# Two layers of attention and feed-forward on one core: the first chunk scored without rows over DRAM, weights folded on column tiles, late weights as steps, a low-rank product on row tiles

## Chip, core and metric

One core of a Trainium2 chip runs the whole program in one launch. The metric is device time in microseconds (us), the median of some runs. TensorE is called PE below, VectorE DVE, ScalarE ACT, GpSimd POOL, and SP is the sync engine, which here only issues DMAs.

## The reference, cut to what matters

The input is 16 sequences of 256 tokens with 128 features. Four stages follow one another, each with a residual and a layer norm: A0 (causal attention, 16 heads of 8 dimensions, queries and keys from low-rank products), F0 (a gated feed-forward of width 512 with two hidden layers), A1 (attention without mask), F1 (a feed-forward in which a router picks one of 8 low-rank additions).

```
q = einsum('bhtr,hrd->bhtd', einsum('btd,hdr->bhtr', x, q_a), q_b)   # rank 64, k alike
att = softmax(where(causal, q @ k.T / sqrt(8), min)); y = att @ v
x = layernorm(x + y @ o_w.T + o_b)                                   # A0
h = silu(x @ w1.T * s1) * (x @ w2.T * s2)
h = gelu(h @ h1.T * t1); h = gelu(h @ h2.T * t2)
x = layernorm(x + h @ w3.T * s3)                                     # F0
x = layernorm(x + attention(x @ W_qkv + b) @ W_out + b_out)          # A1, no mask
e = argmax(x @ gate_W.T + gate_b)
h = relu(x @ wi.T + wi_b + (x @ A[e].T) @ B[e].T)
x = layernorm(x + h @ wo.T + wo_b)                                   # F1
```

## The kernel before

**Chunks and steps.** A chunk is one sequence of 256 tokens, and each of the four stages handles 16 chunks. Every engine runs a list of steps written out by hand as letters (`SEQUENCE`): `KIND` gives each letter's name and stage, and a letter's n-th use is chunk n. Engines meet through counted semaphores. All PSUM banks are one pool of eight, and `BANK_TABLE` says which bank each step of PE takes, so a step waits until that bank's last user is done.

**Weights at the start.** PE folds the low-rank factors into the two 128x128 matrices `wq`: 16 products, one for a pair of heads and a side (queries, keys), each with a 128x128 stationary operand (`wqa`) and 16 moving columns (`wqb`) (L821). DVE copies the result (L626). ACT issues the DMAs of all other weights at the start, but for `wh` and `w3`, which follow the first chunk's key rows (`key_rows`, L544 to L550).

**Scores in bf16 rows.** Attention scores have a contraction of only 8, and float32 precision is wanted. So `qk` gives q and k for all heads (features by tokens); ACT and DVE split them into three bf16 parts (`split`, L557, L659 to L669); SP parks the parts in a DRAM scratch (`park`, L423) and fetches them back as 72 rows a head (`fetch`: `qrow` L434, `krow` L439), so that one bf16 matmul with 72 rows holds all products of the parts. `pass1` (L874, L883) makes scores with queries on partitions, 3 banks for 4 heads in A0 and 4 in A1, and DVE takes the row maxima (L704, or L695 with the mask from chunk 2 on in A0; in chunks 0 and 1 PE adds the mask, L865). `maxima` turns the maxima (L894), DVE splits them too (L723 to L729), and SP writes them as three more rows of `qrow` (L447). `pass2` (L916) makes the transposed scores less the maximum with 75 rows, ACT takes the exponential (L575), POOL zeroes the diagonal's upper part in A0 (`causal`, L515), and `values` (L934) multiplies by v on four column tiles of 32. For chunk 0 of A0 the maxima and rows go in two halves (`HALVED`, `early`, L902 to L715, L453).

**The rest of a chunk.** `outputs`, `merge`, `project`, `turn` normalise, turn and project; the feed-forward of F0 is `gated` (L985), `hidden` (L1003, half of all its PE work), `down` (L1052). `scale` multiplies F0's weights by their scales on DVE (L636 to L648), once. In F1, `route` (L1014) gives the router's logits and the low-rank values, DVE keeps those of the chosen expert in `low`, `lora` turns them (L1023), and `expert` adds, for each of four blocks of 128 features, the product with `wi` (L1033) and one with `wlb` (L1034). Of the latter's 128 contraction rows only 32 hold weights, the rest are zero.

## Time and profile before

| | |
|---|---|
| median of 3 runs | 928.54 us (925.82 to 929.03) |
| the profiled execution | 927.51 us, span 925.7 us |
| PE busy | 870.4 us, 94% |
| PE weight loads | 689.3 us, 74% |
| DVE busy | 670.8 us, 72% |
| ACT busy | 488.5 us, 53% |
| POOL busy | 185.6 us, 20% |
| DMA | 65.17 MB, mean 70 GB/s |

The span runs from the first to the last instruction; some 1.8 us of the execution's time lie outside it. A busy share counts a matmul from its start to its modelled end, and neighbours overlap, so that PE at 94% is not PE at its peak. A float32 matmul shows as two records and a bf16 one as one, so counts of float32 matmuls in the views are double those in the code.

### The profile page before, as it was taken

What the parts mean: (1) busy time and instruction counts of PE and PEld (TensorE: products, weight loads), DVE (VectorE), ACT (ScalarE), POOL (GpSimd) and SP (SyncE); (2) the same over time, 40 slices, a digit from 0 to 9 for tenths busy, and PEclk for the clock granted to TensorE, in tenths of its full rate; (3) what the DMA queues carried; (4) which work ended last, traced back from release to release, by engine and by line L of the source; (5) the groups of instructions that cost most, each with busy time, mean ns of one, the idle gap of its engine ahead of it and who ended that gap; (6) DMA issues with size and microseconds to landing.
All of it is one profiled execution on the core that took longest, in us unless ns stands there. A gap on an engine that the chain in (4) does not pass through costs nothing.

```text
span 925.7 us, 19247 instructions
## 1 busy us (share of the span) xinstructions
PE 870.4 (94%) x7076; PEld 689.3 (74%) x7076; DVE 670.8 (72%) x2379; ACT 488.5 (53%) x951; POOL 185.6 (20%) x389
## 2 busy tenths in 40 slices
PE   5589899999999999999999999999999999999996
PEld 4358687876777876688777887778867888787855
DVE  5767658749998579964799659965899659654863
ACT  1143454376655545645547665646565665562372
POOL 2132221003400233002320034002320114010211
PEclk9879899999999999999999999999999999999999
DMA  7613031402322034301252023400442022002200
GB/s 243 205 47 104 20 98 53 126 13 60 105 71 77 1 93 129 87 2 37 68 145 76 2 70 113 116 10 1 118 115 71 7 75 65 13 8 63 81 15 12
DMA packets 49044, 65.17 MB, mean 70 GB/s; under 512 B 5624, under 2 KB 42744, under 8 KB 44248
## 3 DMA queue, kind: packets, MB, share of 16 engines
q1 hardware_dynamic: 46552, 58.02, 21.9%
q10 hardware_dynamic: 2400, 5.93, 1.9%
q8 instruction: 57, 0.93, 0.4%
q14 instruction: 35, 0.29, 0.1%
HBM read 48.46 MB, written 14.68 MB: 68 GB/s over the span
## 4 chain that ended last, share of the span: by engine, by line
PE 65%; DVE 12%; DMA 11%; issue 4%; ACT 4%; SPq 3%; POOL 1%; ACTq 0%; POOLq 0%; DVEq 0%
PE banks L1003 19%; PE banks L916 8%; PE banks L934 8%; DMA krow<-scratch 7%; PE banks L883 6%; PE banks L985 5%; PE banks L1052 4%; DVE top L704 3%; PE banks L838 2%; DMA scratch<-split 2%; DMA qrow<-tsplit 2%; SPq L439 1%; PE banks L874 1%; PE banks L1033 1%; PE banks L1034 1%
## 5 line engine op out<-in xcount | busy, mean ns | idle before, releaser
L575 ACT ACTIVATE prob<-banks 128x384 f32<-128x384 f32 (+1 forms) x512 | 247.0, 550 | 117.2 <-PE banks L916 97.4
L704 DVE TENSOR_REDUCE top<-banks 128x2 f32<-128x512 f32 (+1 forms) x280 | 176.0, 680 | 38.5 <-PE banks L883 27.9
L695 DVE CUSTOM_DVE_ANT_0 banks<-banks,above 128x128 f32<-128x128 f32 x448 | 145.5, 388 | 42.0 <-PE banks L883 29.6
L916 PE MATMUL banks<-qrow,krow 75*128 75x256 bf16 (+1 forms) x1024 | 155.6, 266 | 8.6 <-ACT prob L575 3.9
L883 PE MATMUL banks<-krow,qrow 72*128 72x256 bf16 x768 | 133.9, 277 | 9.2 <-DVE top L704 5.0
L916 PEld LDWEIGHTS banks<-qrow,krow 75*128 75x128 bf16 x1024 | 89.5, 100 | 47.0 <-ACT prob L575 11.2
L934 PE MATMUL banks<-prob,v 128*32 128x256 f32 (+1 forms) x2048 | 122.8, 367 | 0.7 <-POOL prob L515 0.6
L508 POOL TENSOR_TENSOR ln_rstd<-ln_var,minus_half 128x2 f32<-128x2 f32 x64 | 44.8, 703 | 380.6 <-DVE ln_var L764 380.3
L1003 PE MATMUL banks<-glu,wh 128*128 128x256 f32 x512 | 116.5, 381 | 1.0 <-ACT prob L575 1.0
L1003 PE MATMUL banks<-hid,wh 128*128 128x256 f32 x512 | 115.9, 380 | 0.0
L1003 PEld LDWEIGHTS banks<-glu,wh 128*128 128x128 f32 x512 | 94.9, 190 | 13.8 <-ACT prob L575 1.2
L1003 PEld LDWEIGHTS banks<-hid,wh 128*128 128x128 f32 x512 | 95.1, 190 | 12.7 <-ACT hid L597 0.5
L883 PEld LDWEIGHTS banks<-krow,qrow 72*128 72x128 bf16 x768 | 68.7, 99 | 33.9 <-DVE top L704 7.1
L934 PEld LDWEIGHTS banks<-prob,v 128*32 128x32 f32 x2048 | 56.6, 111 | 48.5 <-issue 18.1
L597 ACT ACTIVATE hid<-banks 128x512 f32<-128x512 f32 x64 | 38.2, 597 | 86.8 <-PE banks L1003 86.4
L515 POOL TENSOR_SCALAR_AFFINE_SELECT prob<-prob 128x512 f32<-128x512 f32 x128 | 81.9, 639 | 0.0
L513 POOL TENSOR_TENSOR pool_carrier<-minus_half 128x1 f32<-128x1 f32 x128 | 29.5, 230 | 242.2 <-ACT prob L575 241.6
L695 DVE DVE_READ_ACCUMULATOR2_ANT top<- 128x1 f32 x448 | 62.4, 139 | 0.0
L985 PE MATMUL banks<-xt,w 128*128 128x256 f32 x256 | 62.2, 389 | 0.0
L503 POOL TENSOR_TENSOR resid<-x,rows 128x256 f32<-128x256 f32 x48 | 34.9, 727 | 113.4 <-DVE ln_sum L751 104.7
L575 ACT ACT_TABLE_LOAD x35 | 44.9, 1283 | 16.6 <-PE banks L916 15.9
L985 PEld LDWEIGHTS banks<-xt,w 128*128 128x128 f32 x256 | 47.4, 194 | 6.8 <-ACT prob L575 0.4
(100 smaller groups left out, 1164.1 us busy)
## 6 DMA issues: line engine op xcount, KB each, us to landing
qrow<-scratch SPq DMA_DIRECT2D x30, 576.0 KB
krow<-scratch SPq DMA_DIRECT2D x90, 192.0 KB
scratch<-split SPq DMA_DIRECT2D x96, 128.0 KB, 1.9
xt<-in_xt SPq DMA_DIRECT2D x16, 128.0 KB, 2.4
x<-in_x SPq DMA_DIRECT2D x16, 128.0 KB, 2.7
wh<-in_wh ACTq DMA_DIRECT2D x2, 1024.0 KB, 8.5
out<-xout SPq DMA_DIRECT2D x16, 128.0 KB, 2.0
qrow<-tsplit SPq DMA_DIRECT2D x90, 8.0 KB
```

What stands on the lines that cost most here:

```text
L508: nc.gpsimd.tensor_tensor(ln_rstd[s][:], ln_var[s][:], minus_half[:], ALU.pow).then_inc(rstd[s], 1)
L515: nc.gpsimd.affine_select(out=diag, in_=diag, compare_op=ALU.is_ge, fill=0.0, base=0, pattern=[[0, 2], [0, QB], [1, P]], channel_multiplie ...
L575: nc.scalar.activation(prob[s][:, j % 2, g, 0:wide], banks[:, b, 0:wide], ACT.Exp, scale=1.0 / float(np.sqrt(np.float32(HD))) if s == A0 e ...
L597: nc.scalar.activation(hid[layer][:, 2 * m:2 * m + 2, :].rearrange("p m t -> p (m t)"), banks[:, g, :], ACT.Gelu).then_inc(gelued, 1)
L695: done = nc.vector.tensor_tensor_reduce(out=bank[:, g * wide:(g + 1) * wide], in0=bank[:, g * wide:(g + 1) * wide], in1=above[:, 2 * P - w ...
L704: nc.vector.tensor_reduce(out=dst, in_=src, axis=AX, op=ALU.max, negate=True).then_inc(maxed[s], 1)
L883: done = nc.tensor.matmul(at, queries(h, qb), keys(h, 2), start=True, stop=not masked, skip_group_check=True)
L916: done = nc.tensor.matmul(bank[:, kb * SEQ:(kb + 1) * SEQ - q0], krow[s][n % DEEP[s]][0:ROWSM, h, kb * P:(kb + 1) * P], qrow[s][n % DEEP[s ...
L934: done = nc.tensor.matmul(banks[32 * i:32 * i + 32, g, q0:SEQ], v[s][:, kb, GROUP * j + i, :], prob[s][:, j % 2, i, kb * SEQ:(kb + 1) * SE ...
L985: done = nc.tensor.matmul(banks[:, g, i * TOK:(i + 1) * TOK], w12[:, side, (2 * m + i) * P:(2 * m + i + 1) * P], xt[F0][n % AHEAD][:], sta ...
L1003: done = nc.tensor.matmul(banks[:, g, i * TOK:(i + 1) * TOK], wh[:, layer, k, (2 * m + i) * P:(2 * m + i + 1) * P], (glu, hid[0])[layer][: ...
L1052: done = nc.tensor.matmul(banks[:, g, t * D:(t + 1) * D], src[:, k, t * P:(t + 1) * P], w[:, k, :], start=k == 0, stop=k == HB - 1)
```

## The change

**First chunk of A0.** It no longer goes over DRAM. The folded weights are spread so that each head has 8 of 32 columns (`wex`), and four products a side give q and k of all heads with one head in 8 of each 32 partitions (L936). `qf` holds the queries of four heads at once; `kf[g]` holds only head g's keys, with zeros elsewhere and a one in a spare row, so that a float32 matmul with 128 rows gives one head's scores (L997, L1001; pass 2 L1065). The maxima are put into that spare row by `shift`: PE turns them and DVE adds them into `qf`. No split, park, fetch or rows of maxima remain for this chunk; chunk 1 is the first to be parked.

**Fold.** `wqb` is stationary (32 columns, padded with zeros) and `wqa` moves (128 columns), on four column tiles. The result is transposed, so it is copied, turned by PE (L928) and copied again. The input `qk_b` is twice as large.

**Late weights.** `late` is a step on ACT in three parts: scales and `w12`; `wh` and `w3`; all others. The first two stand ahead of all exponentials, the third behind six of them. DVE's memsets of `krow` are on POOL.

**Park and fetch.** Queries and keys have scratches of their own, the keys' in the order in which they are read. A park is six DMAs and was three; a fetch of keys is still three, each from one run of DRAM.

**Low-rank product.** `wlb` holds the 32 rows of weights twice, at partitions 0 and 32, and DVE writes `low` twice. An `expert` step now covers the whole chunk: all four products with `wi` first, ahead of the wait for `lowt`, then the four with `wlb`, each with 32 rows, alternating between the two row tiles and two banks.

**Order.** All five lists and the bank table are new throughout.

```diff
-HALVED = {A0: 0, A1: CHUNKS - 1}
+HALVED = {A0: None, A1: CHUNKS - 1}
+EARLY = {A0: 0, A1: CHUNKS - 1}
@@ SEQUENCE, pe: first line, before and after
-        "abaccccccccdcccceeefeeeeeggceccceeceecececcecccggbfhaijeeeeeeeeegeeekegeeesggbhcscaicctcjccccctcctfkcccc"
+        "aaaaaaabcaadeaeaeeeeafeegeeeefeeeeaaaaaafaaafaaahacgidjeeeeeeeekeefeeeeeferffchaaaridaaajsaasaakaaarrgasaa"
@@ pe, start
-            pe.wait_ge(weights0, 2 * DMA)
-            for pair in range(HEADS // 2):
-                if pair == HEADS // 4:
-                    pe.wait_ge(weights0b, DMA)
-                for side in range(2):
-                    at = banks[:, 0, side * D:(side + 1) * D].rearrange("p (c h) -> p c h", h=HEADS)[:, :, 2 * pair:2 * pair + 2]
-                    done = nc.tensor.matmul(at, wqa[:, pair, side, :],
-                                            wqb[:, pair, side, :].rearrange("p (c h) -> p c h", h=2), start=True, stop=True)
-            done.then_inc(folded, 1)
+            for half in range(2):
+                if half == 0:
+                    pe.wait_ge(weights0, 2 * DMA)
+                else:
+                    pe.wait_ge(weights0b, DMA)
+                for side in range(2):
+                    for i in range(4):
+                        pair = 4 * half + i
+                        done = nc.tensor.matmul(banks[32 * i:32 * i + 32, half, side * D:(side + 1) * D], wqb[:, pair, side, :],
+                                                wqa[:, pair, side, :], start=True, stop=True, skip_group_check=True)
+                done.then_inc(folded, 1)
             pe.wait_ge(made, 2)
+            for half in range(2):
+                pe.wait_ge(kept, half + 1)
+                for side in range(2):
+                    done = nc.tensor.transpose(banks[:, 2 + half, side * D:(side + 1) * D], turned[:, half, side * D:(side + 1) * D], ident[:])
+                done.then_inc(unturned, 1)
+            pe.wait_ge(wex_ready, 2)
+            pe.wait_ge(loaded[0], 2 * DMA)
+            for half in range(2):
+                for side in (1, 0):
+                    for i in range(2):
+                        done = nc.tensor.matmul(banks[:, 5 + 2 * half - side, i * TOK:(i + 1) * TOK], wex[:, side, 2 * half + i, :], xt[A0][0][:],
+                                                start=True, stop=True)
...
@@ pe, pass1
+                if s == A0 and is_first(n):
+                    for g in range(GROUP):
+                        if u == 0:
+                            at = bank[:, g * P:(g + 1) * P]
+                            nc.tensor.matmul(at, qf[:, j, 0:P], kf[g][:, j, 0:P], start=True, stop=False, skip_group_check=True)
+                            done = mask(at)
...
@@ dve, start
+            for half in range(2):
+                dve.wait_ge(folded, half + 1)
+                nc.vector.tensor_copy(turned[:, half], banks[:, half, 0:2 * D]).then_inc(kept, 1)
...
+            def shift(half, g):
+                at = qf[:, 2 * half:2 * half + 2].rearrange("p j t -> p (j t)")
+                nc.vector.tensor_tensor(at, at, banks[:, g, :], ALU.add).then_inc(shifted, 1)
@@ act
+            def late(s, n, k):
+                if k == 0:
+                    act.dma_start(early[:, HEADS * D:HEADS * D + 4 * HID], d_in["scales"].partition_broadcast(P)).then_inc(weights2, DMA)
+                    act.dma_start(w12[:], d_in["w12"]).then_inc(weights2, DMA)
+                elif k == 1:
+                    for layer, there in enumerate((weights3, weights4)):
+                        act.dma_start(wh[:, layer], d_in["wh"][:, layer]).then_inc(there, DMA)
+                    act.dma_start(w3raw, d_in["w3"]).then_inc(weights4, DMA)
...
@@ sp, park
-                    sp.dma_start(scratch[s][n % 2][:, i].rearrange("a p t -> p a t"), split[s][:, i]).then_inc(parked[s][n % 2], DMA)
+                    sp.dma_start(scratch[s][n % 2][i], split[s][:, i, 0]).then_inc(parked[s][n % 2], DMA)
+                    sp.dma_start(kscratch[s][n % 2][:, i], split[s][:, i, 1]).then_inc(parked[s][n % 2], DMA)
@@ pe, expert
-            def expert(s, n, m, g):
-                if m == 0:
-                    pe.wait_ge(lora_done, 1 * n + 1)
-                last.wait(pe, g)
+            def expert(s, n, ga, gb):
+                for pair, g in enumerate((ga, gb)):
+                    last.wait(pe, g)
+                    for i in range(2):
+                        m = 2 * pair + i
+                        nc.tensor.matmul(banks[:, g, i * TOK:(i + 1) * TOK], wi[:, m * P:(m + 1) * P], xt[F1][n % AHEAD][:],
+                                         start=i == 0, stop=False, skip_group_check=True)
+                pe.wait_ge(lora_done, 1 * n + 1)
                 for i in range(2):
-                    at, cut = banks[:, g, i * TOK:(i + 1) * TOK], slice((2 * m + i) * P, (2 * m + i + 1) * P)
-                    nc.tensor.matmul(at, wi[:, cut], xt[F1][n % AHEAD][:], start=True, stop=False)
-                    done = nc.tensor.matmul(at, wlb[:, cut], lowt[:], start=False, stop=True)
+                    for pair, g in enumerate((ga, gb)):
+                        m, tile = 2 * pair + i, slice(pair * ER, (pair + 1) * ER)
+                        done = nc.tensor.matmul(banks[:, g, i * TOK:(i + 1) * TOK], wlb[tile, m * P:(m + 1) * P], lowt[tile],
+                                                start=False, stop=True, skip_group_check=True)
```

PE's first instructions before: the fold (`inter` and `prob` hold `wqb` and `wqa` at that time), q and k of chunks 0 and 1, and the first scores of chunk 0.

```order
L821 MATMUL banks<-inter,prob 128x8x2 [waits weights0]
...
L821 MATMUL banks<-inter,prob 128x8x2 [waits weights0b]
...
L838 MATMUL banks<-xt_0,wq 128x256 [waits loaded_0,wready,made]
...
L847 MATMUL banks<-wv,xt_0 128x128 [waits weights1]
...
L838 MATMUL banks<-xt_1,wq 128x256 [waits parts0,loaded_1]
...
L874 MATMUL banks<-krow_0,qrow_0 128x128 [waits parts0,half_spread0]
```

And in the changed kernel (`glu` holds the folded weights to be turned, `hid` holds `wex` and then `qf`, `qrow` of A1 holds `kf`):

```order
L921 MATMUL banks<-prob,inter 32x128 [waits weights0]
...
L921 MATMUL banks<-prob,inter 32x128 [waits weights0b]
...
L928 MATMUL banks<-ident,glu 128x128 [waits kept,made]
...
L928 MATMUL banks<-ident,glu 128x128 [waits kept]
...
L936 MATMUL banks<-xt_0,hid 128x256 [waits loaded_0,wex_ready]
L936 MATMUL banks<-xt_0,hid 128x256 x7
L997 MATMUL banks<-qrow_0,hid 128x128 [waits wready,qkf_made,kf_made]
```

The first scores now wait for copies on ACT and DVE and not for rows from DRAM; v of chunk 0 and q and k of chunk 1 come behind them.

PE at the very end of the program before, the last chunk's expert step and what stands just ahead of it:

```order
L1052 MATMUL banks<-wout,inter 128x128 x8
L1023 MATMUL banks<-ident,low 128x128 x2
L1033 MATMUL banks<-xt_1,wi 128x256
L1034 MATMUL banks<-lowt,wlb 128x256
L1033 MATMUL banks<-xt_1,wi 128x256
L1034 MATMUL banks<-lowt,wlb 128x256
```

The same place in the changed kernel:

```order
L1211 MATMUL banks<-wout,inter 128x128 x8
L1175 MATMUL banks<-ident,low 128x128 x2
L1184 MATMUL banks<-xt_1,wi 128x256 x4
L1191 MATMUL banks<-lowt,wlb 128x256 x4
L1211 MATMUL banks<-wout,inter 128x128 x8
```

The four products with `wi` moved ahead of all four with `wlb`, and of the wait for `lowt`.

SP's queue before, from the first loads to chunk 1's rows:

```order
L423 DMA scratch0_0<-split0 128x2x256 x3
L409 DMA xt0_0<-in_xt 128x256
L410 DMA x0_0<-in_x 128x2x128
L434 DMA qrow0_0<-scratch0_0 72x1x2048 x2
L423 DMA scratch0_1<-split0 128x2x256 x3
L453 DMA qrow0_0<-tsplit0 1x8x256 x3
L434 DMA qrow0_1<-scratch0_1 72x1x4096
L439 DMA krow0_1<-scratch0_1 24x1x4096 x3
```

The same place in the changed kernel, where each of the three parts is now two DMAs (two of the three pairs are left out):

```order
L462 DMA scratch0_1<-split0 128x256
L463 DMA kscratch0_1<-split0 8x16x256
...
L478 DMA qrow0_1<-scratch0_1 72x1x4096
L483 DMA krow0_1<-kscratch0_1 24x4096 x3
L450 DMA xt0_0<-in_xt 128x256
L451 DMA x0_0<-in_x 128x2x128
```

Chunk 0's park, fetch and rows of maxima are gone from the queue, and chunk 1's are the first in it.

## Rows read from the trace of the kernel before

**Rows 1.** The page: its head and busy times.
```profile
span 925.7 us, 19247 instructions
PE 870.4 (94%) x7076; PEld 689.3 (74%) x7076; DVE 670.8 (72%) x2379; ACT 488.5 (53%) x951; POOL 185.6 (20%) x389
...
PEclk9879899999999999999999999999999999999999
```

**Rows 2.** Timeline of PE: start us, us, instruction, [idle before <-releaser].
```profile
5.44 7.01 PE L821 MATMUL banks<-inter,prob 128*128 128x16 f32 x32 [5.44 <-DMA prob<-in_qk_a]
13.02 2.04 PE L838 MATMUL banks<-xt,wq 128*128 128x256 f32 x4 [0.56 <-issue]
...
28.29 0.29 PE L874 MATMUL banks<-krow,qrow 72*128 72x128 bf16 x1 [9.61 <-DMA krow<-scratch]
...
33.39 0.42 PE L883 MATMUL banks<-krow,qrow 72*128 72x256 bf16 x1
33.60 0.31 PE L865 MATMUL banks<-above,identb 128*128 128x128 bf16 x1
...
34.82 0.22 PE L874 MATMUL banks<-krow,qrow 72*128 72x128 bf16 x1
34.88 0.22 PE L865 MATMUL banks<-above,identb 128*128 128x128 bf16 x1
...
39.42 0.39 PE L883 MATMUL banks<-krow,qrow 72*128 72x256 bf16 x1 [3.97 <-DVE top L704]
...
56.42 1.51 PE L934 MATMUL banks<-prob,v 128*32 128x256 f32 x32
```

**Rows 3.** Timeline of all engines: DVE scales `wh`.
```profile
36.35 2.29 DVE L648 TENSOR_TENSOR wh<-wh,prob 128x2048 f32<-128x2048 f32 x1
```

**Rows 4.** Groups by line and form: busy us, mean ns | idle before.
```profile
L704 DVE TENSOR_REDUCE top<-banks 128x2 f32<-128x512 f32 x272 | 171.3, 680 | 28.8 <-PE banks L883 27.9 <-PE banks L865 0.3
...
L575 ACT ACTIVATE prob<-banks 128x384 f32<-128x384 f32 x256 | 111.2, 495 | 72.4 <-PE banks L916 57.4 <-PE banks L934 14.3
...
L1034 PE MATMUL banks<-lowt,wlb 128*128 128x256 f32 x128 | 38.8, 386 | 0.0
...
L804 DVE TENSOR_TENSOR low<-banks,pick 128x64 f32<-128x64 f32 x16 | 3.6, 224 | 0.6
```

**Rows 5.** Timeline of PE at a `values` step on four column tiles.
```profile
207.03 1.07 PE L934 MATMUL banks<-prob,v 128*32 128x256 f32 x16
208.03 0.71 PE L847 MATMUL banks<-wv,xt 128*128 128x128 f32 x4
```

**Rows 6.** Stretches: us, PE, PEld, DVE, ACT, POOL busy (x), clock, DMA share, GB/s.
```profile
210.00:290.00 80.00, 77.15 (x751) 55.94 (x752) 75.07 (x281) 50.83 (x116) 21.79 (x45) 1.00 0.30 87
...
141.00:142.00 1.00, 1.00 (x11) 1.00 (x11) 1.00 (x8) 1.00 (x1) 0.00 (x0) 1.00 0.89 279
146.00:147.00 1.00, 1.00 (x18) 0.66 (x11) 0.90 (x2) 0.29 (x1) 0.00 (x0) 1.00 0.43 139
800.00:926.00 126.00, 114.36 (x843) 90.25 (x841) 67.44 (x220) 55.94 (x111) 14.00 (x20) 0.97 0.11 33
```

**Rows 7.** Stretch of L1034's instructions alone: PE, PEld, clock, DMA share, GB/s.
```profile
800.00:926.00 126.00, 12.66 (x40) 8.18 (x40) 0.97 0.11 33
```

**Rows 8.** Timeline of all engines: one park of three DMAs on SP's queue.
```profile
134.70 2.67 SPq L423 DMA_DIRECT2D scratch<-split  x3
```

**Rows 9.** Timeline of the last chunk's expert and down steps.
```profile
914.22 0.70 PE L1033 MATMUL banks<-xt,wi 128*128 128x256 f32 x2 [0.47 <-ACT lowt L602]
...
917.78 0.61 PE L1052 MATMUL banks<-wout,inter 128*128 128x128 f32 x4
917.98 0.84 ACT L610 ACTIVATE inter<-banks,cols 128x256 f32<-128x256 f32 x2 [0.89 <-PE banks L1034]
918.87 1.60 PE L1052 MATMUL banks<-wout,inter 128*128 128x128 f32 x12 [0.48 <-ACT inter L610]
```

More of the change, by code:

```diff
@@ L168, in parts_of @@
             "scale": [(k,) for k in range(4)],
+            "late": [(k,) for k in range(3)],
             "gated": [(m,) for m in range(PAIRS)],
[L170 to L171 removed]
+            "hidden": [(layer, m) for layer in range(2) for m in range(PAIRS)]}.get(name, [()])
 def sequence(engine):
```

421 lines of the change are left out of this document (260 added, 161 removed).

## The prediction

> **What bounds the kernel now.** I read the page first. TensorE (PE) is busy for 94% of the span, DVE for 72%, all others less [rows 1]. So PE comes first, but a busy share is no peak, so I priced PE's instructions by how far apart their starts lie. A bf16 matmul with 256 columns starts the next one 0.21 us later at 33.39, which is the lower clock level (1.2 GHz), and one with 128 columns 0.06 us later at 34.82, which is the upper (2.4 GHz) [rows 2]. The last expert step runs 16 float32 records of 256 columns between 914.22 and 917.78, so 0.22 us each at the upper level [rows 9]. A float32 matmul is two such records, so it costs four times a bf16 one.
>
> Then the start, in PE's timeline. The fold waits for its weights until 5.4 and takes 7.0 us for 32 records of only 16 columns. q and k of chunk 0 follow at 13.0. Then PE stands for 9.6 us, until the first key rows have come back from DRAM at 28.3. It stands again for 4.0 us ahead of 39.4, where DVE's maxima are late, and DVE is late because it scales `wh` at 36.35 for 2.3 us [rows 2, 3]. Chunk 0's last `values`, with all of chunk 1's `pass1` ahead of it, ends at 56.42 + 1.51 = 57.9 us [rows 2]. That is my mark for the head.
>
> Last, the middle. From 210 to 290 PE is busy 77.2 of 80 us, but DVE 75.1 of 80; from 800 to the end DVE is busy only 67.4 of 126 [rows 6]. So there are stretches in which DVE is as near its limit as PE, and work taken off PE there isn't all gained.
>
> The sums go against the profiled execution, 927.5 us (span 925.7 and 1.8 around it). The median of the runs is 928.5, so 1.0 us is added at the end.
>
> **The head.** The fold's weights are 128 KB more, at 279 GB/s 0.5 us [rows 6]: the first half is there at 5.9, the second (512 KB) at about 7.8. Its 16 records of 128 columns on four column tiles are 4 slots of 0.21 = 0.9 us, and 0.4 of latency: 9.1. Two copies of about 0.4 (half the columns of a DVE reduce of 0.68 [rows 4]) and two turns with latency, 0.8, give 10.7. Then come eight matmuls for q and k, 16 records: 6.9 us at the lower level (0.43 each), 3.5 at the upper. The first scores start between 14 and 17.6; I take 17, since before the change four such records at 13.02 took 2.04 us, the slow rate [rows 2]. ACT's and DVE's copies into `kf` and `qf` (0.5 to 0.6 us each, by [rows 4]) are hidden by the second half of these matmuls. So the first score moves from 28.3 to 17.
>
> But it is dearer. A head has 128 + 256 columns in `pass1` and as many in `pass2`: 0.06 + 0.11 = 0.17 us in bf16, 0.22 + 0.44 = 0.66 in float32. PE's work up to my mark, at the upper level, is: `pass1` of chunk 0 16 x 0.66 and 32 masks of 0.06, 12.5; `pass2` 16 x 0.66, 10.6; v and q and k of chunk 1, 1.3; eight turns of maxima 0.9; four `values` 3.2; chunk 1's `pass1` 16 x 0.17 and masks, 4.6. In all 33.1. DVE's two scalings of `wh` (2.3 each) stand ahead of the last maxima of chunk 0 and delay the second `shift`: 1.4. Chunk 1's 12 maxima take DVE 12 x 0.68 = 8.2 [rows 4], while PE has 6.2 beside them: 2.0. One more us for scores begun at the lower level. 17 + 33.1 + 4.4 = 54.5, against 57.9: **-3.4**. Chunk 1's rows have from its q and k at about 29 to 44 to go over DRAM; before it took 13.02 to 28.3, some 15 us, for the same, so it is just covered. Bounds: -7.5 if the clock is up from the first product and DVE delays nothing, +8 if half of the scores run at the lower level.
>
> **The expert step.** For `wlb` there are 128 records [rows 4], 8 a chunk, of 0.22 each. With two row tiles at a time they are 4 slots: -0.88. The change of tiling costs: at 207.03 16 records on four column tiles are 4 slots, 0.87 us, and the next full matmul starts not at 207.90 but at 208.03 [rows 5]; 0.13 out and about as much in, less what is hidden, 0.2. Net -0.68, times 16 = -10.9. Of the 128 records 40, five chunks, lie behind 800 us [rows 7], where DVE has room: -3.4 in full. The other eleven lie mostly in stretches like 210 to 290, and I count half: -3.7. Together **-7.1**, bounds -10.9 and +2.
>
> The column tiles' row shows four tiles at once: 16 records in 1.0 us, where one after the other they would need 16 x 0.22 = 3.5. No row shows row tiles. The Trainium skill ("TensorE: Matmul & The Clock Gate", section "Measured speedup vs the span model") gives 3.07x for four row tiles, and by it two tiles would overlap as I assume. The Trainium skill also says ("TensorEngine Tiling (Array Packing)", section "Key Properties") that a change of tiling mode drains TensorE; that speaks against this edit, and the gap of 0.13 us at 207.9 agrees.
>
> **The end.** After `lowt` is there (914.2) PE now works 3.6 us, and ACT's last `inter` comes at 917.98 for 0.84, before the last 12 records of `down` start at 918.87 [rows 9]. Now the `wi` products lie ahead, in PE's idle time. After 914.2 there are 0.9 us of `wlb`, 0.3 of latency, and two pairs of ACT copies, 1.7: 917.1. **-1.7**.
>
> **What it adds.** `low` is written twice: 0.22 us x 16 on DVE [rows 4], half of it felt: **+1.8**. A park has three more DMAs; three took 2.67 us in SP's queue, with waits for the parts [rows 8]. Behind them stand fetches, but those have 15 us of other work on PE to hide in. Against this the fetch of keys may be shorter: at 141 the DMA share is 0.89 and at 146, when only keys are left, 0.43 [rows 6], and a source in one run could be spread better. I take 0 for both, bounds -4 and +15 (0.5 us on each of 31 chunks). The memsets moved to POOL are hidden: its first mask is due only behind the first four exponentials. The new order of all lists is 0 by itself; nothing in it shows a price.
>
> Sum: -3.4 - 7.1 - 1.7 + 1.8 = -10.4, so 927.5 - 10.4 = 917.1, and with 1.0 for the median **918 us**.
>
> **Rivals.**
> More than that (908). The head gains 7.5, the expert step all of 10.9, since other work of PE fills the stretches in which DVE is full, and fetches 2: 10.9 + 7.5 + 1.7 + 2 - 1.8 = 20.3, and 927.5 - 20.3 + 1.0 = 908. For it: PE stands idle for 5.4, 9.6 and 4.0 us at the start, 19 in all [rows 2]. Against it: DVE's 75.1 of 80 us [rows 6]. 0.16.
> Row tiles take turns (928). Then the 8 records stay, the switch comes on top: +2 for -7.1, and 0.9 less at the end: 918 + 10 = 928. No row excludes it. The Trainium skill ("TensorE: Matmul & The Clock Gate", section "LDWEIGHTS (loading the stationary operand)") says that a load of 32x128 takes as long as one of 128x128, so that the loads would bound the step if they were not side by side. 0.12.
> Late weights (922). Scales, `w12`, `wh` and `w3` are 3.8 MB, issued from about 17.5 on; at 279 GB/s they land at about 32, and DVE wants the last of them at about 33. A slower rate of 200 GB/s gives 36.5, and DVE stops with maxima behind it: +4. 0.08.
> The clock stays low (940, slower). The fold kept PE busy from 5.4 to 12.4 and q and k behind it still ran at the lower level; the page's clock is 7 tenths in its third slice (46 to 69 us) [rows 1, 2]. If chunk 0's scores in float32, 23 us of work, all run at 1.2 GHz, they cost 23 more: 918 + 23 - 1 = 940. It decides from the point at which some 10 us of that work are run slowly. Against it: scores in bf16, begun at 28.3, ran at the upper level from 34.8 on, after 6 us of dense work [rows 2], and here dense work begins at 10.7. 0.08.
> SP's queue is late (930). 0.4 us on each of 31 parks is felt, 12.4: 918 + 12 = 930. 0.06.
> My forecast has the remaining 0.50, with a range of its own of 911 to 924.
>
> **How the numbers follow.** 0.5% (4.6 us) is about what a measurement of this kernel tells from no change: 923.9 and 933.2 are the borders. Faster: 0.47 of my own, 0.16, and half of the late weights, about 0.66. Same: the row tiles' case, the rest of mine and of the small ones, 0.20. Slower: the low clock and the worst of the queue and the turns, 0.14. 904 to 932 leaves out the low clock and the tails of the two outer cases, less than 2 in 10.
>
> **What would show it.** First score near 17 us and no wait for `krow` there; chunk 1's `pass1` done near 54; pairs of `wlb` records starting within some hundredths of a us; from `lowt` to the last `down` 2.9 us in place of 4.7. I am wrong if records of 256 columns are still 0.43 us apart at 25 us, if the `wlb` records start 0.22 apart, or if PE waits for rows of keys more often in the middle.

## The result, and the profile after

The changed kernel is slower: 955.46 us median (952.23 to 967.0, 4 runs) against 927.18 (919.10 to 929.03, 4 runs) of the kernel before on the same chip. The ratio is 1.0311, 95% interval 1.0229 to 1.0393; the run of 967.0 us was in a slower state of the chip, and the ratio leaves it out. The forecast was 918, range 904 to 932. The profiled execution took 954.73 us, its span is 953.0.

The page's busy times and the granted clock in 40 slices, of the changed kernel:

```profile
PE 889.0 (93%) x7160; PEld 699.1 (73%) x7160; DVE 669.1 (70%) x2393; ACT 480.5 (50%) x948; POOL 197.2 (21%) x395
...
PEclk9889799999999997999989999999999999899989
```

And that of the kernel before, as one stretch over its whole span (PE, PEld, DVE, ACT, POOL busy, clock, DMA share, GB/s):

```profile
0.00:926.00 926.00, 870.45 (x7076) 689.27 (x7076) 670.77 (x2379) 488.54 (x951) 185.62 (x389) 0.98 0.24 70
```

The 27.3 us more of span are of two kinds. TensorE's busy time grew by 18.5 us although work was taken off, and its idle time by 8.8 (953.0 - 889.0 = 64.0, before 925.7 - 870.5 = 55.2). The first goes with the clock: its mean is 0.960 in place of 0.981, which by itself would be (1 - 0.960) x 953.0 - (1 - 0.981) x 925.7 = 20.5 us (an estimate), and the row of slices has dips in the middle where the kernel before has none [rows 1]. The second is small as a sum because the head lost idle time while the middle got more. TensorE's waits in the changed kernel (engine, line, what was waited for: us in total, times, longest us):

```profile
PE banks L1015 <- DMA krow<-kscratch: 22.6, 16, 2.3
...
PE banks L1006 <- DMA krow<-kscratch: 6.1, 5, 1.7
PE banks L1068 <- DMA qrow<-tsplit: 5.1, 5, 2.9
```

L1006 and L1015 are the first scores (`pass1`). They wait 21 times for rows of keys, 28.7 us. The kernel before waited for such rows 9 times and 16.7 us, 9.6 of it once, ahead of the first scores:

```profile
PE banks L874 <- DMA krow<-scratch: 12.9, 4, 9.6
...
PE banks L883 <- DMA krow<-scratch: 3.8, 5, 1.5
```

Without that one, which the change took away, these waits went from 7.1 to 28.7 us. That was one of the signs named beforehand for a wrong forecast.

The head and the end did much of what was forecast. TensorE at the start (start us, us, instruction, [idle before <- releaser]):

```profile
5.80 1.08 PE L921 MATMUL banks<-prob,inter 128*32 128x128 f32 x16 [5.80 <-DMA prob<-in_qk_a]
...
10.80 5.06 PE L936 MATMUL banks<-xt,hid 128*128 128x256 f32 x16 [0.38 <-DVE hid L691]
16.41 0.49 PE L997 MATMUL banks<-qrow,hid 128*128 128x128 f32 x2 [0.56 <-ACT qrow L594]
...
39.35 0.86 PE L1086 MATMUL banks<-prob,v 128*32 128x256 f32 x16 [2.93 <-POOL prob L573]
44.06 4.64 PE L1065 MATMUL banks<-hid,qrow 128*128 128x256 f32 x16 [0.78 <-DVE hid L792]
...
49.42 2.88 PE L1065 MATMUL banks<-hid,qrow 128*128 128x256 f32 x16
...
58.95 0.66 PE L965 MATMUL banks<-wv,xt 128*128 128x128 f32 x4
```

The first score starts at 16.41 (before 28.29 [rows 2]). The two score groups of L1065 with 16 records show the clock: 2.88 us at 49.42, the upper level, 4.64 at 44.06, where part ran at the lower one. Chunk 1's `pass1` is done at 58.95; before, the mark was 57.9. And the end, where the low-rank products run on two row tiles:

```profile
941.82 0.39 ACT L662 ACTIVATE lowt<-banks 128x256 f32<-128x256 f32 x1 [1.91 <-PE banks L1175]
941.62 1.89 PE L1184 MATMUL banks<-xt,wi 128*128 128x256 f32 x8
943.44 1.13 PE L1191 MATMUL banks<-lowt,wlb 32*128 32x256 f32 x8
945.61 2.24 PE L1211 MATMUL banks<-wout,inter 128*128 128x128 f32 x16 [1.03 <-ACT inter L671]
```

Eight records of `wlb` take 1.13 us where eight full ones of `wi` take 1.89. The row tiles do run together. `lowt` is there at 942.21, while the products with `wi` still run, so the `wlb` products at 943.44 wait for TensorE and no longer for `lowt`.

### The profile page after: what moved, and what is told of

It reads as the page before. It is cut to its first block, busy times and chain, and to the rows that moved or that the text cites. A ratio compares the mean times of both kernels' runs of the same rounds, so it can differ in the third digit from the quotient of the medians.

```text
span 953.0 us, 19502 instructions
## 1 busy us (share of the span) xinstructions
PE 889.0 (93%) x7160; PEld 699.1 (73%) x7160; DVE 669.1 (70%) x2393; ACT 480.5 (50%) x948; POOL 197.2 (21%) x395
## 4 chain that ended last, share of the span: by engine, by line
PE 52%; DMA 17%; DVE 16%; SPq 7%; issue 4%; ACT 3%; POOL 1%; POOLq 0%; ACTq 0%; DVEq 0%
PE banks L1155 14%; DMA krow<-kscratch 11%; PE banks L1086 7%; PE banks L1068 7%; PE banks L1015 7%; DVE top L788 4%; PE banks L1137 4%; DMA kscratch<-split 3%; PE banks L1211 3%; DMA qrow<-tsplit 3%; DVE banks L777 2%; SPq L483 2%; SPq L462 1%; SPq L493 1%; PE banks L956 1%
## 5 line engine op out<-in xcount | busy, mean ns | idle before, releaser
L788 DVE TENSOR_REDUCE top<-banks 128x2 f32<-128x512 f32 (+1 forms) x268 | 168.9, 682 | 64.7 <-PE banks L1015 56.2
L1068 PE MATMUL banks<-qrow,krow 75*128 75x256 bf16 x992 | 153.5, 273 | 7.9 <-DMA qrow<-tsplit 5.1
L777 DVE CUSTOM_DVE_ANT_0 banks<-banks,above 128x128 f32<-128x128 f32 x448 | 144.4, 389 | 15.6 <-PE banks L1006 8.4
L1015 PE MATMUL banks<-krow,qrow 72*128 72x256 bf16 x752 | 132.3, 287 | 24.0 <-DMA krow<-kscratch 22.6
L1086 PE MATMUL banks<-prob,v 128*32 128x256 f32 (+1 forms) x2048 | 125.1, 377 | 3.2 <-POOL prob L573 2.9
L1155 PE MATMUL banks<-hid,wh 128*128 128x256 f32 x512 | 118.2, 385 | 0.0
L1015 PEld LDWEIGHTS banks<-krow,qrow 72*128 72x128 bf16 x752 | 69.4, 102 | 50.8 <-DMA krow<-kscratch 27.1
L1086 PEld LDWEIGHTS banks<-prob,v 128*32 128x32 f32 x2048 | 59.0, 114 | 52.3 <-issue 19.2
L573 POOL TENSOR_SCALAR_AFFINE_SELECT prob<-prob 128x512 f32<-128x512 f32 x128 | 85.0, 664 | 0.0
```

Source lines behind the costliest of these rows:

```text
L573: nc.gpsimd.affine_select(out=diag, in_=diag, compare_op=ALU.is_ge, fill=0.0, base=0, pattern=[[0, 2], [0, QB], [1, P]], channel_multiplie ...
L777: done = nc.vector.tensor_tensor_reduce(out=bank[:, g * wide:(g + 1) * wide], in0=bank[:, g * wide:(g + 1) * wide], in1=above[:, 2 * P - w ...
L788: nc.vector.tensor_reduce(out=dst, in_=src, axis=AX, op=ALU.max, negate=True).then_inc(maxed[s], 1)
L1015: done = nc.tensor.matmul(at, queries(h, qb), keys(h, 2), start=True, stop=not masked, skip_group_check=True)
L1068: done = nc.tensor.matmul(bank[:, kb * SEQ:(kb + 1) * SEQ - q0], krow[s][n % DEEP[s]][0:ROWSM, h, kb * P:(kb + 1) * P], qrow[s][n % DEEP[s ...
L1086: done = nc.tensor.matmul(banks[32 * i:32 * i + 32, g, q0:SEQ], v[s][:, kb, GROUP * j + i, :], prob[s][:, j % 2, i, kb * SEQ:(kb + 1) * SE ...
```

## The experiments

All times are medians; each ratio is to runs of the kernel before on the same chip, with its 95% interval. The kernel before had medians of 925.5 to 930.7 us next to the variants, so where two variants are compared below, the difference is that of their ratios times 927 us. Names beginning with a_ start from the changed kernel, names with b_ from the kernel before.

### The layout put back, the order put back, each edit alone

**a_oldlayout**: the changed kernel, its new order kept, with queries and keys in one scratch tensor again.

```
-sp.dma_start(scratch[s][n % 2][i], split[s][:, i, 0])
-sp.dma_start(kscratch[s][n % 2][:, i], split[s][:, i, 1])
+sp.dma_start(scratch[s][n % 2][:, i].rearrange("a p t -> p a t"), split[s][:, i])
...
-        kscratch[s][n % 2].rearrange("c j h t -> (c j) h t")[:, heads]
+        scratch[s][n % 2][1].rearrange("j (c h) t -> c j h t", c=HD)[:, :, heads]
```

> The changed kernel with its new order and all its steps, but parking and fetching as the kernel before does: 3 DMAs for each park instead of 6, one scratch tensor, the key rows read out of it. If the new layout of the rows over DRAM is what makes the rows late (theory B), this gives back most of the loss: 930 to 938 us, and TensorE's waits for krow fall from some 30 us to under 12. If the loss lies in the order, which leaves less work between a chunk's projection and its first scores (theory A), it stays within 5 us of the changed kernel: 950 to 960.

Measured: 924.31 us, ratio 0.9968 (0.9936 to 1.0001). From there to the changed kernel's 1.0311 it is 0.0343, so the layout alone costs some 32 us in the new order. Theory B holds, A falls as it was put. Its profiled execution has a span of 919.2, TensorE busy for 869.5 and a mean clock of 0.982. Against it the changed kernel is busy for 19.5 us more and idle for 14.3 more, 13.4 of them waits for rows of keys (28.7 against 15.3). The other runs say much the same of the clock: over all runs that the ratios use its mean is 0.977 and that of the changed kernel 0.961, a difference of 15 us of span, an estimate. So about half of the 32 us is waiting and about half the clock.

**a_oldorder**: from step 50 of TensorE on, the lists of the kernel before.

> The changed kernel with its code, its new head and its new layout over DRAM, but from step 50 of TensorE on (chunk 0 done up to its last output) all five engines follow the order of the kernel before; the two expert steps of a chunk are one, at the place of the second. Theory A (the new order): back to 915 to 930 us, TensorE's waits for krow at the 10 us or so of before. Theory B (the layout): still over 945, since the rows come as late as now.

Measured: 948.92 us, ratio 1.0252 (1.0187 to 1.0317). The old order does not bring the time back; the joined expert steps in it are a cost of their own, as the next runs show.

**b_newlayout**: the layout alone, in the kernel before (the edit above the other way round).

> The kernel before with one edit: queries and keys parked into two scratch tensors by 6 DMAs for each chunk, and the key rows fetched from the second. Theory A: within 5 us of the kernel before, 922 to 932, since the old order leaves 22 us and more between projection and first scores in stage A0. Theory B: 940 or more. A park that merely starts its last part 0.9 us later would cost 31 times at most that where nothing covers it: 28 us, and nothing where all is covered.

Measured: 945.70 us, ratio 1.0181 (1.0121 to 1.0241). So it costs 17 us in the old order. The 22 us and more of the expectation are there only for A0's chunk 1 and from its chunk 5 on (projection at 165.68, first score at 205.75). From projection to first score chunks 2 to 4 of A0 have some 17 (59.84 to 76.88, and 79.16 to 96.31), and 15 of the 16 chunks of A1 have under 20. So the run doesn't show that the layout costs time where there is room. Of the 13.6 us that its profile is longer, 9.9 stand already at the projection of A1's chunk 1 (170.32 for 160.47).

**b_rowtiles**: the expert step alone.

```
-            "expert": [(m,) for m in range(PAIRS)]}
...
+for i in range(2):
+    for pair, g in enumerate((ga, gb)):
+        m, tile = 2 * pair + i, slice(pair * ER, (pair + 1) * ER)
+        matmul(banks[:, g, i * TOK:(i + 1) * TOK], wlb[tile, m * P:(m + 1) * P], lowt[tile], ...)
```

> The kernel before with one edit: both expert steps of a chunk as one, at the second's place, with the low-rank products last and on two row tiles that run together (wlb and low are held twice). In the trace of the changed kernel 128 such products took 18.1 us busy against 38.8. By the step of the prediction: 10.9 us less TensorE work, of which some 7 come off the time: 918 to 924. If the products are no shorter in the middle, or their time is covered by waits anyway: 925 to 930.

Measured: 947.96 us, ratio 1.0233 (1.0154 to 1.0313), 22 us slower, which neither expectation allowed. **b_merged** asked why.

> b_rowtiles (947.96 us) without the row tiles: the same one expert step a chunk in the order of the kernel before, but the low-rank products on rows 0 to 63 one after the other, one copy of wlb and low. It tells why b_rowtiles was slower than the kernel before. If joining the two steps within an order that was made for two costs the time, this is slower still, 952 to 960. If it was the second load of wlb in the head, or the row tiles themselves, it is near the kernel before: 925 to 932.

Measured: 957.47 us, ratio 1.0342 (1.0289 to 1.0396). Joining the two steps at one place in an order made for two costs some 32 us, and the row tiles give 10 of them back, though the two intervals overlap a little. Why the joined step costs so much no run takes apart: its first half comes later than before, it holds two banks at once, and the bank table around it is another. The profile of b_merged is that of its longest run (966.34 us). Its whole-span stretch shows the price mostly in busy time at a lower clock (897.38 against 870.45), the rest as idle time:

```profile
0.00:965.00 965.00, 897.38 (x7076) 700.38 (x7076) 673.69 (x2379) 486.65 (x951) 185.71 (x389) 0.96 0.23 68
```

One row of it is a warning on marks in single profiles. Nothing in its head is edited, yet chunk 2's projection starts 5.7 us later than in the profile of the kernel before, in the first row here:

```profile
59.84 1.03 PE L838 MATMUL banks<-xt,wq 128*128 128x256 f32 x4
```

```profile
65.58 1.03 PE L840 MATMUL banks<-xt,wq 128*128 128x256 f32 x4
```

In b_newlayout it is 5.6 later too, so the 9.9 us given there are partly of this kind.

**a_onetile**: what the row tiles are worth in the new order, without the layout.

```
-        m, tile = 2 * pair + i, slice(pair * ER, (pair + 1) * ER)
+        m, tile = 2 * pair + i, slice(0, ER)
```

> a_oldlayout with one edit: all low-rank products of the experts on row tile 0 (rows 0 to 63 of wlb and low), so that no two run together. TensorE work grows by the 20.7 us that the busy times of the two forms differ by (38.8 and 18.1), or by the 10.9 of the prediction's step, which took them from start to start. By that step the time grows by some 7 us: 929 to 935. If that work lies under waits for rows, by less than 3: under 927.

(The rows 0 to 63 of the expectation are rows 0 to 31 in the kernel: a tile holds 32.) Measured: 925.77 us, ratio 1.0005 (0.9973 to 1.0038), by the ratios 3.4 us over a_oldlayout, with intervals that overlap. In a_onetile the products take 31.8 us busy instead of 18.1, and the waits for rows are shorter by nearly half of that:

```profile
L1188 PE MATMUL banks<-lowt,wlb 32*128 32x256 f32 x128 | 31.8, 387 | 0.0
...
PE banks L1012 <- DMA krow<-scratch: 5.1, 6, 1.6
...
PE banks L1003 <- DMA krow<-scratch: 3.3, 2, 1.7
```

In a_oldlayout the same two waits are 11.7 and 3.6, 15.3 us in all against 8.4. So about half of the work taken off TensorE came back as waiting for rows, in one execution of each.

### What in the layout costs it

Two parts of it were open: SP issues 6 DMAs for a park, and the keys are read from another tensor.

**a_sixparks**: old tensor and old reading, but six parks.

```
-sp.dma_start(scratch[s][n % 2][:, i].rearrange("a p t -> p a t"), split[s][:, i])
+for a in range(2):
+    sp.dma_start(scratch[s][n % 2][a, i], split[s][:, i, a])
```

> The faster variant a_oldlayout (one scratch tensor, key rows read as before; 924.3 us) with one edit: each of the three parts is parked by 2 DMAs, queries and keys apart, so SP issues 6 for a park instead of 3. In the profiles the last part's issue stood 2.05 us behind the first with 3 DMAs and 2.92 with 6, and the whole way from the first park to the last row 13.5 and 14.4. If it is SP's issuing that makes the rows late (theory B1), this is as slow as the changed kernel: 945 to 958. If it is the reading from the second tensor (its 8 KB packets took 0.53 us against 0.46; theory B2), it stays at 922 to 930.

Measured: 944.30 us, ratio 1.0205 (1.0138 to 1.0273). Six parks alone bring 22 of the 32 us. The other 10 are left for the new tensor, though the intervals of this and of the changed kernel overlap a little.

**a_onekey**: the changed kernel with one DMA for the keys of all three places.

```
-for i in range(PARTS):
-    sp.dma_start(krow[...][i * HD * PARTS:(i + 1) * HD * PARTS, heads], kscratch[...](c j) ...)
+sp.dma_start(krow[...][0:ROWS, heads], kscratch[...](c j) ... .unsqueeze(0).to_broadcast([PARTS, PARTS * HD, ...]))
```

> The changed kernel, new layout and 6 parks, with one edit that only this layout allows: the key rows of all three places come with one DMA instead of three, so SP issues 2 for a fetch instead of 4 (some 0.98 us less between first and last issue). B1: the way is as short again as in a_oldlayout, 920 to 932. B2: the rows are still read slowly, 945 or more. If one DMA of 576 KB is spread over fewer engines at a time than three of 192 KB, it may be slower than 955 too.

Measured: 1071.78 us, ratio 1.1581 (1.1527 to 1.1634). Two issues less, and 118 us more than the changed kernel. TensorE waits 98.2 us for keys:

```profile
PE banks L1014 <- DMA krow<-kscratch: 71.2, 16, 5.6
PE banks L1005 <- DMA krow<-kscratch: 27.0, 7, 5.4
```

The last us of a fetch, in a stretch of a_onekey and one of the changed kernel (the two numbers at the end are DMA share and GB/s):

```profile
414.00:421.00 7.00, 2.17 (x38) 1.43 (x30) 2.65 (x10) 2.15 (x6) 0.00 (x0) 1.00 0.38 122
```

```profile
361.00:367.00 6.00, 4.28 (x53) 2.70 (x51) 4.15 (x17) 2.23 (x6) 0.00 (x0) 1.00 0.82 182
```

The same bytes move with a share of 0.38 instead of 0.82: the one DMA used fewer of the 16 engines at a time. The Trainium skill ("DMA: Bandwidth & Descriptors", section "Why a DMA increments its semaphore by 16 and not by 1") says that a DMA runs on the largest number of engines up to 16 that divides the slowest dimension of both sides. By it the slowest dimension of 3 in a_onekey gives three engines, 24 rows give twelve, and the new key parks (slowest dimension 8) run on eight where the old parks had sixteen. The traces agree. Where only the one DMA of keys moves (417.5 to 418.5 in a_onekey), the share is 0.19 (3 of 16); in the changed kernel's fetch it is 0.74 at 360 (12 of 16 would be 0.75). While a park of keys moves alone it is 0.53 (353.6 to 353.9), and 0.99 in a park of a_oldlayout (345.9 to 346.1). a_oldlayout's key rows, with a slowest dimension of 8 at their source, come at 0.48 (355.0 to 355.4; 8 of 16 would be 0.50). So the new tensor made the fetch of keys wider and their parks narrower.

**a_tiny**: the issues without the rows, in a_oldlayout.

```
+tiny = nc.dram_tensor("tiny", [PARTS, 1, 16], F32, kind="Internal").ap()
 ...
 sp.dma_start(scratch[s][n % 2][:, i]..., split[s][:, i])
+sp.dma_start(tiny[i], ident[0:1, 0:16])
```

> a_oldlayout (924.3 us) with one edit: behind each of the 3 parks of a chunk SP issues one more DMA, of 64 bytes into a tensor of its own, and the fetch waits for those too. Queries and keys move exactly as in a_oldlayout. If SP's issuing is what made a_sixparks (944.3) slower, this is as slow: 940 to 948. If it was the smaller transfers, it stays at 922 to 928.

Measured: 930.03 us, ratio 1.0048 (1.0012 to 1.0084), 7 us over a_oldlayout, between the two expectations: of the 22 us of a_sixparks the issues alone bring a third. They do it without longer waits: in a_tiny's profile TensorE is idle for 48.4 us and in a_oldlayout's for 49.7, but busy for 8.9 more at a mean clock of 0.972 in place of 0.982. How three small DMAs bring that about is open. SP's queue at the park and fetch of the same chunk shows what the four have in common. First the changed kernel, then a_oldlayout, a_sixparks and a_tiny (of each its first park and its fetch of queries):

```profile
351.83 0.35 SPq L462 DMA_DIRECT2D scratch<-split  x1
352.22 0.58 SPq L463 DMA_DIRECT2D kscratch<-split  x1
...
356.87 0.81 SPq L478 DMA_DIRECT2D qrow<-scratch  x1
357.72 1.35 SPq L483 DMA_DIRECT2D krow<-kscratch  x3
```

```profile
343.59 2.41 SPq L460 DMA_DIRECT2D scratch<-split  x3
347.46 0.79 SPq L475 DMA_DIRECT2D qrow<-scratch  x1
348.29 2.05 SPq L480 DMA_DIRECT2D krow<-scratch  x3
```

```profile
353.02 3.07 SPq L461 DMA_DIRECT2D scratch<-split  x6
357.30 0.81 SPq L476 DMA_DIRECT2D qrow<-scratch  x1
```

```profile
345.49 0.36 SPq L461 DMA_DIRECT2D scratch<-split  x1
...
349.41 0.82 SPq L477 DMA_DIRECT2D qrow<-scratch  x1
```

From the first park to the fetch it is 3.87 us in a_oldlayout, 3.92 in a_tiny, 4.28 in a_sixparks and 5.04 in the changed kernel, and the kernels stand in the same order: 0, 7, 22 and 32 us over a_oldlayout. This is one chunk of 31 (A1's chunk 5), so it gives the order and no price. Keys' issues take 0.7 less in the changed kernel (1.35 for 2.05), and its fetch of keys is wider, but neither is felt: from the fetch's first issue to the first scores it is 9.74 us in the changed kernel (356.87 to 366.61) and 9.76 in a_oldlayout (347.46 to 357.22). The whole difference of this chunk lies ahead of the fetch, in the parks. TensorE for that chunk, changed kernel, a_oldlayout and a_tiny:

```profile
366.61 0.61 PE L1015 MATMUL banks<-krow,qrow 72*128 72x256 bf16 x4 [1.72 <-DMA krow<-kscratch]
368.32 0.88 PE L1068 MATMUL banks<-qrow,krow 75*128 75x256 bf16 x4 [1.10 <-DMA qrow<-tsplit]
```

```profile
357.22 0.61 PE L1012 MATMUL banks<-krow,qrow 72*128 72x256 bf16 x4 [0.56 <-DMA krow<-scratch]
358.96 0.61 PE L1065 MATMUL banks<-qrow,krow 75*128 75x256 bf16 x4 [1.13 <-DMA qrow<-tsplit]
```

```profile
358.93 0.61 PE L1014 MATMUL banks<-krow,qrow 72*128 72x256 bf16 x4 [0.38 <-DMA krow<-scratch]
360.65 0.61 PE L1067 MATMUL banks<-qrow,krow 75*128 75x256 bf16 x4 [1.11 <-DMA qrow<-tsplit]
```

A wait of 1.72 in place of 0.56, each with a second of 1.1 behind it, and then the clock. Stretches of the changed kernel behind them, and one of a_oldlayout (the number ahead of the DMA share is the granted clock):

```profile
370.00:374.00 4.00, 4.00 (x23) 2.62 (x24) 2.30 (x5) 2.56 (x5) 0.00 (x0) 0.50 0.61 172
374.00:378.00 4.00, 4.00 (x27) 2.06 (x23) 2.33 (x5) 1.09 (x2) 0.00 (x0) 0.50 0.56 123
378.00:382.00 4.00, 4.00 (x28) 2.00 (x26) 1.98 (x3) 1.72 (x4) 0.00 (x0) 0.50 0.00 0
```

```profile
361.00:365.00 4.00, 4.00 (x44) 2.68 (x42) 3.66 (x9) 3.21 (x8) 0.00 (x0) 1.00 0.69 195
```

For these 12 us TensorE has the lower level, 1.2 GHz, and does 78 instructions where a_oldlayout does 134 in as long (361 to 373). That costs about 6 us; the wait itself cost 1.2. Together they make this the dearest chunk of all: its projection starts 8.2 us later than in a_oldlayout (349.79 for 341.56), A0's projection behind it 15.6 later (383.90 for 368.28), 7.4 of the 33.8 us between the two spans.

But the longer wait isn't shown to be what lowered the clock. In a_tiny the waits are the shortest of the three, 0.38 and 1.11, and the granted clock is 0.50 from 362 to 370 all the same. And the changed kernel's longest wait for keys, 2.30 us ahead of 150.66, has a clock of 1.00 from 150 to 162 behind it.

### Room in the order, and versions that are faster

**a_early** and **a_oldlayout_early**: A0's projections stand earlier in all lists (the tables alone; shown for chunk 6 on TensorE, d is the projection, the other letters are other steps).

```
-efeeefeAeAAeeAHiAed
+defeeefeAeAAeeAHiAe
```

> The changed kernel with its layout and 6 parks; one edit, in the tables: stage A0's projections (qk) of chunks 2 to 15 stand 2 to 18 steps of TensorE earlier, which puts 3.1 to 5.2 us more of TensorE's work between a chunk's projection and its first scores (chunk 5 stays), on ACT, VectorE and SP as far forward as the order of the other steps allows. If the loss is a way over DRAM that is 0.9 us longer in an order with nothing to spare (the theory as it now stands), the waits for krow fall from 28.7 us to under 15 and the time to 920 to 935. If the rows come late because SP or the split engines are behind, whatever the order, it stays above 945.

> The same earlier projections with the old layout and its 3 parks. Theory as it stands: its waits for krow, 15.3 us without the earlier projections, fall under 8, and the time from 924.3 to 910 to 920, faster than both kernels. If what is left of the waits has other causes (maxima, masks), no change: 922 to 927. If the order of the other engines suffers from the steps put forward, it is slower than 927.

Measured: 988.89 us, ratio 1.0710 (1.0645 to 1.0774), and 959.31 us, ratio 1.0356 (1.0305 to 1.0408). Both 36 to 37 us slower than without the edit. Waits for krow did fall, in the first at L1015 from 22.6 to 15.0 us; new ones took their place, for maxima, layer-norm sums and parts on VectorE (here for maxima):

```profile
PE banks L1033 <- DVE top L785: 6.8, 4, 5.0
PE banks L1012 <- DMA krow<-scratch: 5.7, 6, 1.6
```

(a_oldlayout_early.) The theory said that more room makes it faster, and the runs don't bear it out. They don't refute it either: the steps could not be moved alone, since the other engines' lists and the bank table changed with them.

**a_oldorder_oldlayout** differs from a_oldlayout by the order alone.

> a_oldorder (948.9 us: new head, row tiles, but the order of the kernel before from step 50 of TensorE on, its two expert steps of a chunk joined) with the old layout and 3 parks. It differs from a_oldlayout (924.3 us) by the order alone, and from b_rowtiles (948.0 us) by the head alone. If the new order, not the new code, is what makes up for the joined expert steps, it is 940 to 950, some 20 us over a_oldlayout, and below b_rowtiles by the 3 us or so that the head gains. If the new head and the row tiles were what paid, it is near 925. The layout's price in this order is then the rest to 948.9.

Measured: 940.11 us, ratio 1.0104 (1.0071 to 1.0138). By the ratios it is 13 us over a_oldlayout, 12 under b_rowtiles and 14 under a_oldorder: with joined expert steps the new order is worth 13, the new head 12, and the layout costs 14 in this order. Each carries some 4 to 8 us of the intervals.

**a_scale**: a_oldlayout with VectorE's scalings of `wh` (v) behind the turned maxima (g).

```
-"aaaaaaabvaacadavvagvaaaaaaaaaaaahgcdj...
+"aaaaaaabvaacadaagvvvaaaaaaaaaaaahgcdj...
```

> a_oldlayout (924.3 us) with one edit: VectorE's two scalings of wh (2.28 us each at 33.20 and 35.40 in its profile) come behind the turned maxima of chunk 0 instead of ahead of them. While they run, GpSimd's mask of the first values takes 2.70 us instead of 0.64 and its carrier 1.96 instead of 0.19, and TensorE waits 2.93 us for it at 38.23. If the scalings hold GpSimd up, the mask takes its usual time, that wait goes, and all later marks come 2 to 3.5 us earlier: 921 to 923, over 0.5% below the kernel before. If GpSimd is late for another reason, the wait stays and the time is 924 to 926. VectorE stood idle 6.5 us from 42.5 on, so the scalings should find room there.

Measured: 923.83 us, ratio 0.9939 (0.9908 to 0.9970), faster than the kernel before. The medians of the kernel before differ, so the ratio, not the median, compares it with a_oldlayout's 0.9968: 3 us, with intervals that overlap, so the trace shows what moved and the time doesn't show what it is worth. GpSimd (POOL) in a_oldlayout and, below, in a_scale:

```profile
33.57 1.96 POOL L568 TENSOR_TENSOR pool_carrier<-minus_half 128x1 f32<-128x1 f32 x1 [1.43 <-ACT prob L632]
35.48 2.70 POOL L570 TENSOR_SCALAR_AFFINE_SELECT prob<-prob 128x512 f32<-128x512 f32 x1
```

```profile
34.47 0.19 POOL L568 TENSOR_TENSOR pool_carrier<-minus_half 128x1 f32<-128x1 f32 x1 [1.43 <-ACT prob L632]
34.60 0.64 POOL L570 TENSOR_SCALAR_AFFINE_SELECT prob<-prob 128x512 f32<-128x512 f32 x1
...
41.86 2.70 POOL L570 TENSOR_SCALAR_AFFINE_SELECT prob<-prob 128x512 f32<-128x512 f32 x1
```

The slow mask went with the scalings to another place, and TensorE's wait of 2.93 became one of 1.83 at 44.61.

**a_halves**: a_scale with every chunk's rows fetched in two pieces of 8 heads.

```
-pieces = 2 if n == HALVED[s] else 1
+pieces = 2
...
+if j == 0 and u == 0 and not (s == A0 and is_first(n)):
+    pe.wait_ge(half_spread[s][n % 2], NSPREAD * turn_of(s, n))
-elif j == (HALVES if n == HALVED[s] else 0) and u == 0:
+elif j == HALVES and u == 0:
     pe.wait_ge(spread[s][n % 2], NSPREAD * turn_of(s, n))
```

> a_scale (ratio 0.9939 to the kernel before) with one edit: every chunk's rows are fetched in two pieces of 8 heads (8 DMAs instead of 4), and the first half of its scores waits for the first piece alone; until now only the last chunk of A1 did so. The first piece should be there some 3 us before the whole was, so the waits for krow, 12.9 us in a_scale, fall under 4, and the time by 8 to 20 us: 902 to 915. If SP's queue pays for the 4 more issues a chunk (0.45 us each, 31 times) as it did in a_sixparks, the rows of maxima and the next parks come later and it is slower than the kernel before: 935 to 950.

Measured: 918.86 us, ratio 0.9914 (0.9876 to 0.9952), the fastest version here, though it is only 2 us under a_scale by the ratios, with intervals that overlap, and short of the 902 to 915 expected. The waits for keys are gone but for one, and a good part came back as waits for the rows of maxima, which SP issues behind the fetches:

```profile
PE banks L1066 <- DMA qrow<-tsplit: 11.3, 8, 4.0
...
PE banks L1013 <- DMA krow<-scratch: 1.1, 1, 1.1
```

## Why the prediction was wrong

**The step that failed** is in "What it adds": "Behind them stand fetches, but those have 15 us of other work on PE to hide in ... I take 0 for both, bounds -4 and +15 (0.5 us on each of 31 chunks)". Measured: +32 in the new order, +17 in the old. Two things were mis-sized. The way over DRAM takes about as long as the work that covers it, so there was hardly any room to hide in: the changed kernel waits for keys at 21 of its 31 trips. In the chunk shown TensorE's projection starts at 349.79 and its scores wait at 366.61, 16.8 us later; before the change 15 us had been measured for the way in the head, and "15 us of other work" should have read as covering it exactly, not as a reserve. And no term stood for TensorE's clock, which took about half of the 32 us; in the chunk shown it took 6 us next to 1.2 of longer waiting. The parks of keys, which now run at a DMA share of 0.53, it did not look at. The rival "SP's queue is late" (930, 0.06) had the right place. It was too small: 0.4 us a park where the chunk shown has 1.2 more between park and fetch, and no term for the clock.

**"A source in one run could be spread better"** (-4) was not seen: in the chunk shown the fetch of keys used more engines, and the rows came no sooner behind it (9.74 us for 9.76). The one fetch that used the new tensor's shape fully, a_onekey, was far slower.

**The new order "is 0 by itself; nothing in it shows a price"** was wrong in the other direction. With the same code it is worth 13 us against the old lists with joined expert steps. Those 32 us that b_merged loses are the price of the expert step's new form in an order not made for it, which the forecast had not considered; the new order makes up for most of them. What in the order does so no run takes apart.

**The expert step, -7.1.** The mechanism was right: row tiles overlap, 1.13 us for eight records, and the rival that they take turns falls. The size in time was not: 3.4 us by a_onetile, within its uncertainty nothing, in the order that the change has, and 10 in the order of b_merged and b_rowtiles. I had let VectorE be the limit in the middle and counted half. In the profiles half of the work does come back, but as waits for rows.

**The head, -3.4.** First score at 16.41 (forecast 17), clock at the upper level there, so that rival falls too. The mark came at 58.95 instead of 54.5. Of the 4.4 us, 2.93 are the wait for GpSimd's mask at 39.35, for which the sum had no term of its own; 1.8 are the score group of 4.64 us, partly at the lower level behind that wait, where the upper took 2.88. The term for the two `wh` scalings was right in its cause and too small, since they hold up GpSimd as well. Without the layout the head paid more than forecast: a_oldorder_oldlayout is 12 us under b_rowtiles, with an uncertainty of 8.

**The end, -1.7.** From `lowt` to the start of the last `down` group it takes 3.4 us (942.21 to 945.61), where 2.9 was forecast and 4.7 measured before. The products with `wi` don't all fit into the idle time: they run 1.2 us beyond `lowt`. And the last group now has 16 records, not 12, so from `lowt` to its end it is 5.6 us for 6.3 before: 0.6 gained for 1.7. No run isolates it.

**Late weights** cost nothing that shows: none of TensorE's or VectorE's costliest waits is for them, and VectorE scales `w12` at 26.32 and `wh` at 34.33.

With the layout taken out, all the other terms together gave a_oldlayout, at a ratio of 0.9968: 3 us of the 10.4 forecast, with an interval that just reaches no change.

**Left open.** How the 32 us part between the issuing (7 by a_tiny), the smaller and more transfers (15 more by a_sixparks) and the new tensor (10, within the intervals) is only roughly told. That waiting and the clock have about half each is read from one execution each and from mean clocks. What lowers the clock in one kernel and not in another with like waits is not shown. Whether more room in the order would help if all steps were planned anew was not tried.

## What to carry to other kernels

When a round trip is covered by just as much work as it takes, a term of 0 for anything on that path is the wrong default: bound it by its full length on every trip (here 1.2 us x 31 = 36, an estimate), and look at TensorE's clock besides. Cutting TensorE work in such a kernel buys less than the work, since part of the saved time turns into waiting for the same transfer. Starting on the first half of the data (a_halves) took the waits for keys away and won 2 us, within the intervals. Before a test in another order is read as one with room, measure that room chunk by chunk. An order planned for one form of a step is part of that form: neither joining two steps nor moving one forward by hand came out even.

## What the runs showed of the hardware

- In the chunk shown, waits of 1.72 and 1.10 us close together were followed by 12 us at 1.2 GHz, though TensorE was fully busy in them; so were waits of 0.38 and 1.11 in a_tiny, by at least 8. Waits of 0.56 and 1.13 at the same place in a_oldlayout left the clock at the upper level, and so did one of 2.30 elsewhere. The length of the last waits alone doesn't tell them apart.
- GpSimd's mask took 2.70 us instead of 0.64 while VectorE multiplied `wh` by `prob`, two inputs in SBUF. It followed the scalings when they were moved. The Trainium skill ("SBUF — State Buffer", section "Who interferes with whom") says that a VectorE instruction with two SBUF inputs contends with a GpSimd instruction that reads SBUF; this trace agrees.
- One DMA of 576 KB for three copies of 24 rows landed later than three of 192 KB: TensorE's waits for keys grew from 28.7 to 98.2 us, the longest from 2.3 to 5.6. Its DMA share alone was 0.19.
- Two row tiles of 32 x 256 columns in float32 really run side by side: 18.1 us busy for 128 records, 31.8 on one tile.
